# A hand-ordered transformer block with 6,700 pieces in another order: due times per tile and layer

## Chip, core and metric

The kernel runs on one core of one Trainium2 chip. The metric is the device time of one execution in microseconds. A run of the kernel before was measured three times; its median is what a change is compared with.

## What is computed

The input x is 8 sequences of 1024 rows of 256 numbers, in float32. Cut to what matters, the reference is:

```
h = layernorm(x) * (1 + ca) + sa                 # ca, sa, ga, ... from silu(c) @ wmod, per sequence
x = x + ga * attention(h)                        # q, k, v by small products; rope; causal softmax over 1024 rows
h = layernorm(x) * (1 + cb) + sb
for l in range(2):                               # two layers
    s = shift_token(h)                           # columns 128..255 come from the row before
    q, k, v = split(s @ wqkv[l])                 # 8 heads of 64
    q, k = rotary_xpos(l2norm(q) * qs, l2norm(k) * ks)
    h = h + local_attention(q, k, v) @ wo[l]     # windows of 128 rows, each sees itself and the one before
    s = layernorm(shift_token(h)) * lg + lb
    a, g = split(s @ w1[l] + b1[l])
    h = h + (a * gelu(g)) @ w2[l] + b2[l]
x = x + gb * h
```

`shift_token` is the part that the change's DMA edit touches: row r of the second half of the columns is taken from row r - 1.

## The kernel before

A batch is one of the 8 sequences; it is cut into 8 tiles ("windows") of 128 rows. For each batch the kernel runs the causal attention tile by tile, then layer 0, then layer 1 over its 8 windows. Window n counts over everything: n = (2 x batch + layer) x 8 + w. L is 2 x batch + layer, p is a pair of windows (0 to 3).

All work is cut into named pieces, and each engine's program is a list of pieces that it executes strictly in that order. A piece waits for the semaphores of what it reads and of what still reads its buffer, and everything behind it on the engine waits with it. The pieces that matter here:

- Window chain. TensorE: E (three blocks: q, k, v of one window, six float16 matmuls each), F (transposes of q and k), G (scores), H (transposes of probabilities), I (probabilities times v), J (output product). ACT: ev (copy of E out of PSUM), sq, fc, ex (exp), hc, oh. VectorE: x0, x1 (rotary products, L752 and L760), ss (L729), tm (mask and scale, L771), nm (normalisation, L780 and L787), hv (copy, L795), ol (L801), jr (residual add, L807). POOL: pw (power, L889), ad (L893), kk (L899).
- Second half of a layer, by pairs. SP: xs copies the residual's second half of the columns, moved down one row, into the tile XS (L276: 127 rows; L278: the one row that comes from the neighbouring tile). VectorE: ls (statistics, L814 to L819) reads XS, POOL: lt (root, L241 and L243), VectorE: lk (normalised rows XN, L828 and L830), TensorE: N (transposes, L293), ACT: nh, VectorE: nl. Then Wg and Wa (first product), ge, us, uh, ul, and Y (second product, 18 matmuls), yr. D, dh, dl transpose the rows for the next layer.
- Attention. SP: xl loads x. VectorE: st, rw (L627), af; POOL: rt, hl, ra; TensorE: pp (L305), pj, qt, sc, pt, av; VectorE: rp (rope), mx, pc, ys, l2, lr (L710 and L714); POOL: r2.

`schedule()` makes the lists. It gives each piece a due time: the time of its tile (ATTN_TILE, WIN_TILE, MLP_BLOCK, Y_TILE) and an offset of its kind (PAIR_AT, ATTN_AT, WIN_AT, LN_AT, D_AT, MLP_AT), the same for all tiles. Sorting by due time gives each engine's list. The due times have no other use but one: `plan_banks()` goes through TensorE's list and gives each piece the PSUM bank (of 8) whose last user is due to be emptied first. TensorE waits in `claim` until that bank has been emptied. The end of a batch's layer 1 and the attention of the next batch are mixed.

Of the kernel before, what the change touches and what calls it, by code (L numbers as in the profile page):

```python
# [22 lines left out]
P = 128  # L23
EPS = 1e-5
BIG = 1.0e30
BATCH, SEQ, DIM = 8, 1024, 256
NT = SEQ // P
# [4 lines left out]
DEPTH = 2  # L32
# [12 lines left out]
def adaln_kernel(nc, x, w_q, w_k, w_v, wqkv, q_scale, k_scale, wo, ln_g, ln_b, w1, b1, w2, b2,  # L45
# [3 lines left out]
    with ExitStack() as ctx:  # L49
# [29 lines left out]
        X, U = xu[:, 0], xu[:, 1]  # L79
# [27 lines left out]
        uh = [mlp[:, 512 * j:512 * j + 256].bitcast(F16) for j in range(NJ)]  # L107
        ul = [mlp[:, 512 * j + 256:512 * j + 512].bitcast(F16) for j in range(NJ)]
# [9 lines left out]
        ra = ar_c[:, 2048:3072].rearrange("p (r c s n) -> p r c s n", r=2, c=NC, s=2)  # L118
        rb = ar_c[:, 3072:4096].rearrange("p (r c s n) -> p r c s n", r=2, c=NC, s=2)
        XN = sb("XN", [P, 2, 2, DIM])  # L120
        XS = sb("XS", [P, NT, P])
        ot = [sb(f"ot_{s}", [P, 4, P], F16) for s in ("hi", "lo")]
        small = sb("small", [P, 160])
        ss = small[:, 0:32].rearrange("p (r n) -> p r n", r=2)
# [18 lines left out]
        s_xs = [sem(f"shifted_rows{p}") for p in range(DEPTH * NT // 2)]  # L143
# [103 lines left out]
        with block:  # L247

            @block.sync
            def _(sp):  # L250
                for piece in ORDER["sp"]:
                    k = piece[0]
                    if k == "xl":
                        b, p = piece[1:]
                        if b:
                            sp.wait_ge(s_fin, (b - 1) * NT + 2 * p + 2)
                        sp.dma_start(X[:, 2 * p:2 * p + 2, :],
                                     x[b, 2 * p * P:(2 * p + 2) * P, :].rearrange("(t p) d -> p t d", p=P)
                                     ).then_inc(s_x[p], 16)
                    elif k == "mb":  # L260
                        b = piece[1]
                        if b:
                            sp.wait_ge(s_u0, at("lr", b - 1, NT - 1))
                        sp.dma_start(modb[:, :, :],
                                     mod_rows[b, 2 * DIM:5 * DIM].rearrange("(k d) -> k d", k=3).partition_broadcast(P)
                                     ).then_inc(s_mod, 16)
                    elif k == "mg":
                        b = piece[1]
                        if b:
                            sp.wait_ge(s_fa, b * NT)  # L270
                        sp.dma_start(modg[:, :], mod_rows[b, 5 * DIM:6 * DIM].partition_broadcast(P)).then_inc(s_modg, 16)
                    elif k == "xs":
                        n = piece[1]
                        l, w = n // NT % DEPTH, n % NT
                        sp.wait_ge(s_res, at("jr", n))
                        sp.dma_start(XS[1:P, w, :], U[0:P - 1, w, P:DIM]).then_inc(s_xs[l * 4 + w // 2], 16)  # L276
                        if w:
                            sp.dma_start(XS[0:1, w, :], U[P - 1:P, w - 1, P:DIM]).then_inc(s_xs[l * 4 + w // 2], 16)  # L278
                    elif k == "os":
                        b, w = piece[1:]  # L280
                        sp.wait_ge(s_fin, b * NT + w + 1)
                        sp.dma_start(out[b, w * P:(w + 1) * P, :], U[:, w, :]).then_inc(s_out[w], 16)
                for w in range(NT):
                    sp.wait_ge(s_out[w], 16 * NB)

# [623 lines left out]


NB = BATCH

ATTN_TILE = [-0.56, 0.47, 18.59, 31.5, 40.69, 48.66, 54.04, 58.53]
WIN_TILE = [5.09, 15.87, 30.06, 42.77, 56.53, 69.72, 82.93, 95.11]
MLP_BLOCK = [[45.88, 47.36, 49.69, 51.6, 54.17, 56.41], [47.05, 51.59, 53.77, 55.46, 58.12, 61.25]]
Y_TILE = [[65.88, 68.27, 88.1, 92.91], [66.34, 67.28, 73.41, 81.93]]
WIN_START = 8.18
NEXT_WIN = 8.61
NEXT_ATTN = 37.34
PAIR_AT = {"rt": ("pool", -17.04), "st": ("dve", -16.46), "rw": ("dve", -13.71), "pp": ("pe", -13.45),  # L920
           "af": ("dve", -11.85), "hh": ("act", -11.2), "hl": ("pool", -9.56)}
ATTN_AT = {"pj": ("pe", -7.22), "rp": ("dve", -6.0), "vc": ("act", -4.93), "ra": ("pool", -3.82),
           "qt": ("pe", -0.96), "qc": ("act", 0.06), "sc": ("pe", 4.46), "mx": ("dve", 6.39), "pe": ("act", 7.34),
           "av": ("pe", 19.13), "ys": ("dve", 21.78)}
PT_AT = (("pt", "pe", 12.02), ("pc", "dve", 15.4))
LN2_AT = {"l2": ("dve", 23.01), "r2": ("pool", 23.88)}
WIN_AT = {("E", 0): ("pe", -4.18), ("E", 1): ("pe", -2.62), ("E", 2): ("pe", -0.89), ("ev", 0): ("act", -0.67),
# [12 lines left out]
LN_AT = {"ls": ("dve", 38.22), "lt": ("pool", 39.18), "lk": ("dve", 41.9), "N": ("pe", 42.57), "nh": ("act", 43.6),  # L940
         "nl": ("dve", 43.85)}
D_AT = {"D": ("pe", 0.87), "dh": ("act", 4.08), "dl": ("dve", 4.31)}
MLP_AT = {"ge": ("act", 1.8), "us": ("dve", 2.88), "uh": ("act", 3.32), "ul": ("pool", 5.78)}
LR_AT = 27.76
YR_AT = 2.17
D_LAG = -0.53


def schedule():

    made = []

    def put(time, engine, *piece):
        made.append((time, engine, piece))

    a, fin = 30.0, [float(p) for p in range(NT // 2)]
    for b in range(NB):
        A = [a + d for d in ATTN_TILE]
        for p in range(NT // 2):
            put(fin[p], "sp", "xl", b, p)  # L960
            for k, (e, d) in PAIR_AT.items():
                put(A[2 * p] + d, e, k, b, p)
            for k, (e, d) in LN2_AT.items():
                put(A[2 * p + 1] + d, e, k, b, p)
# [4 lines left out]
        for t in range(NT):  # L969
            for k, (e, d) in ATTN_AT.items():  # L970
                put(A[t] + d, e, k, b, t)
            for k, e, d in PT_AT:
                for k4 in range(t // 4 + 1):
                    put(A[t] + d + 0.9 * k4, e, k, b, t, k4)
        s = a + ATTN_TILE[NT - 1] + WIN_START
        d_time = [A[2 * p + 1] + LR_AT + 2.5 for p in range(NT // 2)]
        for l in range(DEPTH):
            L = b * DEPTH + l
            S = [s + d for d in WIN_TILE]
            for p in range(NT // 2):  # L980
# [4 lines left out]
            for w in range(NT):  # L985
                for key, (e, d) in WIN_AT.items():
                    put(S[w] + d, e, key[0], L * NT + w, *key[1:])
            d_time = []
            for g in range(NG):
                m = S[GW * g + GW - 1]  # L990
                for j in range(NJ + 1):
                    put(m + MLP_BLOCK[g][j], "pe", "Wg", L, g, j)
                    if j < NJ:
                        put(m + MLP_BLOCK[g][j] + 1.3, "pe", "Wa", L, g, j)
                    for k, (e, d) in MLP_AT.items():
                        put(m + MLP_BLOCK[g][j] + d, e, k, L, g, j)
                for i in range(GW):
                    y, n = m + Y_TILE[g][i], L * NT + g * GW + i
                    put(y, "pe", "Y", n)
# [6 lines left out]
                if g == 0:  # L1006
                    s_next, a_next = m + Y_TILE[0][0] + NEXT_WIN, m + Y_TILE[0][0] + NEXT_ATTN
            s = s_next
        a = a_next
    made.sort(key=lambda q: q[0])  # L1010
    return ({e: [q for _, g, q in made if g == e] for e in ("sp", "pe", "act", "dve", "pool")},
            {q: time for time, _, q in made})

# [363 lines left out]
```

## Time and profile before

| | |
|---|---|
| median of 3 runs | 3347.26 us (3340.87 to 3353.93) |
| the profiled execution: time, span | 3337.88 us, 3336.1 us |
| granted TensorE clock, mean | 0.939 |
| busy: TensorE, VectorE, ACT, POOL | 2891.3, 2513.0, 1812.7, 1312.5 us |
| instructions: TensorE, VectorE, ACT, POOL | 21580, 7195, 4165, 949 |

All times of a trace are counted from the start of the span. Setup (weights split into a high and a low float16 part) takes the first 110 us or so; then the batches follow at about 400 us each.

### The profile page before, as it was taken

How to read it: one execution, taken by the hardware profiler on the slowest of the kernel's cores; microseconds unless marked ns; L12 is line 12 of the kernel's file. 1: busy time of each engine (PE TensorE's matmuls, PEld its weight loads, DVE VectorE, ACT ScalarE, POOL GpSimd, SP SyncE). 2: the span in 40 equal slices, each digit the busy share in tenths (PEclk: the TensorE clock that was granted, in tenths of full speed). 3: DMA queues.
4: the chain of work that ended last, by engine and by line, in shares of the span. 5: the costliest groups of instructions: out<-in, count | busy, mean ns of one | idle time of the engine just before them, and what ended most of it. 6: DMA issues, size and time to landing. Idle time of an engine off the chain costs nothing.

```text
span 3336.1 us, 63227 instructions
## 1 busy us (share of the span) xinstructions
PE 2891.3 (87%) x21580; PEld 2009.4 (60%) x21580; DVE 2513.0 (75%) x7195; ACT 1812.7 (54%) x4165; POOL 1312.5 (39%) x949
## 2 busy tenths in 40 slices
PE   2489988899888998899979899789988899888997
PEld 2266665666566665566656666566665666556665
DVE  3588777878678786887868878688777978678785
ACT  2146653567536674366734666346653557536673
POOL 1234433544335443344423444344433544335442
PEclk9799999999999999999989999899999999999998
DMA  4100000000000000000000000100000000000000
GB/s 140 33 3 6 4 13 25 4 5 5 22 15 4 5 5 22 14 5 5 5 28 8 5 5 6 33 3 5 5 13 25 4 5 4 22 15 5 4 5 16
DMA packets 57885, 46.22 MB, mean 14 GB/s; under 512 B 18438, under 2 KB 54876, under 8 KB 57444
## 3 DMA queue, kind: packets, MB, share of 16 engines
q1 hardware_dynamic: 53520, 35.14, 3.6%
q10 hardware_dynamic: 4052, 7.04, 0.6%
q8 instruction: 181, 2.97, 0.4%
q14 instruction: 132, 1.08, 0.1%
HBM read 25.33 MB, written 8.44 MB: 10 GB/s over the span
## 4 chain that ended last, share of the span: by engine, by line
PE 55%; DVE 22%; DMA 9%; issue 5%; POOL 3%; ACT 1%; SPq 1%; DVEq 0%; POOLq 0%; ACTq 0%
PE ps L134 11%; PE ps L135 10%; PE ps L136 10%; DMA XS<-xu 8%; PE ps L425 5%; PE ps L410 5%; PE ps L399 4%; DVE ar_b L771 4%; PE ps L334 3%; PE ps L293 2%; DVE small L729 2%; DVE ar_b L787 2%; DVE ar_c L752 2%; PE ps L385 2%; PE ps L353 1%
## 5 line engine op out<-in xcount | busy, mean ns | idle before, releaser
L889 POOL TENSOR_TENSOR small<-small,neg_half 128x16 f32<-128x16 f32 x128 | 391.2, 3056 | 644.5 <-DVE small L734 643.6
L562 ACT ACTIVATE ar_b<-ar_b,small 128x256 f32<-128x256 f32 (+1 forms) x1024 | 492.6, 482 | 113.5 <-DVE small L771 112.0
L771 DVE CUSTOM_DVE_ANT_0 ar_b<-ps,mask_t,small 128x256 f32<-128x256 f32 (+1 forms) x1024 | 413.0, 461 | 12.0 <-PE ps L399 12.0
L410 PE MATMUL ps<-id_f,ar_b 128*128 128x128 f32 x1920 | 280.1, 295 | 102.4 <-DVE ar_b L787 102.3
L787 DVE TENSOR_SCALAR ar_b<-ar_b,rsw 128x256 f32<-128x256 f32 (+1 forms) x1024 | 342.4, 396 | 9.3 <-DVE rsw L780 0.2
L241 POOL TENSOR_SCALAR stats<-stats 128x2 f32<-128x2 f32 x128 | 35.5, 277 | 769.2 <-DVE stats L819 332.7
L410 PEld LDWEIGHTS ps<-id_f,ar_b 128*128 128x128 f32 x1920 | 233.2, 151 | 153.3 <-DVE ar_b L787 137.6
L844 DVE SCALAR_TENSOR_TENSOR mlp<-ps,bias,mlp 128x512 f32<-128x512 f32 x192 | 143.7, 748 | 233.7 <-ACT mlp L592 108.2
L893 POOL TENSOR_TENSOR ar_c<-ar_c 128x1024 f32<-128x1024 f32 x128 | 301.1, 2352 | 20.5 <-DVE ar_c L760 20.5
L908 POOL TENSOR_TENSOR mlp<-mlp 128x512 f16<-128x512 f32 x160 | 193.2, 1208 | 268.3 <-ACT mlp L601 267.3
L134 PE MATMUL ps<-wqkv_hi,ht_hi 128*128 128x512 f16 x768 | 295.9, 385 | 0.0
L135 PE MATMUL ps<-wqkv_lo,ht_hi 128*128 128x512 f16 x768 | 294.8, 384 | 0.0
L136 PE MATMUL ps<-wqkv_hi,ht_lo 128*128 128x512 f16 x768 | 294.2, 383 | 0.0
L134 PE MATMUL ps<-ht_hi,w_hi 128*128 128x512 f16 (+1 forms) x704 | 273.1, 388 | 1.4 <-DVE ht_lo L724 1.4
L135 PE MATMUL ps<-ht_lo,w_hi 128*128 128x512 f16 (+1 forms) x704 | 271.5, 386 | 0.0
L136 PE MATMUL ps<-ht_hi,w_lo 128*128 128x512 f16 (+1 forms) x704 | 269.9, 383 | 0.0
L399 PE MATMUL ps<-ar_a 64*128 64x128 f32 x3840 | 262.8, 289 | 6.8 <-ACT ar_a L552 6.8
L425 PE MATMUL ps<-ar_b,ar_a 128*64 128x128 f32 x3840 | 257.5, 289 | 1.2 <-ACT ar_b L571 1.1
L399 PEld LDWEIGHTS ps<-ar_a 64*128 64x128 f32 x3840 | 236.9, 196 | 33.1 <-issue 24.6
L425 PEld LDWEIGHTS ps<-ar_b,ar_a 128*64 128x64 f32 x3840 | 224.8, 146 | 32.7 <-issue 27.2
L552 ACT ACTIVATE ar_a<-ps 128x512 f32<-128x512 f32 x256 | 148.1, 595 | 104.1 <-PE ps L385 104.0
L571 ACT ACTIVATE ar_b<-ps 128x512 f32<-128x512 f32 (+1 forms) x256 | 144.7, 568 | 100.6 <-PE ps L410 99.5
(171 smaller groups left out, 6837.8 us busy)
## 6 DMA issues: line engine op xcount, KB each, us to landing
xu<-in_L_attn_x_dram SPq DMA_DIRECT2D x32, 256.0 KB, 3.0
out_dram<-xu SPq DMA_DIRECT2D x64, 128.0 KB, 1.7
XS<-xu SPq DMA_DIRECT2D x128, 63.5 KB
ar_a<-in_L_ffn_wqkv_dram ACTq DMA_DIRECT2D x1, 3072.0 KB, 17.1
modb<-mod_rows SPq DMA_DIRECT2D x8, 384.0 KB, 3.5
XS<-xu SPq DMA_DIRECT2D x112, 0.5 KB
ar_a<-in_L_wmod_dram SPq DMA_DIRECT2D x1, 1536.0 KB, 7.5
xu<-in_L_ffn_w_dram SPq DMA_DIRECT2D x1, 1364.0 KB, 9.4
```

The costliest lines, as they stand in the source:

```text
L134: pe.matmul(o, a[0], b[0], start=start, stop=False)
L135: pe.matmul(o, a[0], b[1], start=False, stop=False)
L136: return pe.matmul(o, a[1], b[0], start=False, stop=stop)
L399: last = pe.matmul(ps[:, bk[q], o:o + P], QT[r:r + 64, n % 2, hp, :], KT[r:r + 64, (n - 1 + kb) % 3, hp, :], start=True, stop=True)
L410: last = pe.transpose(ps[:, bk, o:o + P], PW[:, f, q, i, kb * P:(kb + 1) * P], id_f[:])
L425: last = pe.matmul(ps[64 * q:64 * q + 64, bk, (h // 2) * P:(h // 2 + 1) * P], V[:, (n - 1 + kb) % 4, h * DH:(h + 1) * DH], PTW[:, f, q, 2 ...
L562: last = act.activation(pw, pw, ACT.Exp, bias=mnw[:, n % 2, h:h + 1], scale=-1.0, accum_out=smw[:, n % 2, h:h + 1])
L771: last = dve.tensor_tensor_reduce(out=PW[:, f, q, i, c:2 * P], in0=ps[:, bk, i * 256 + c:(i + 1) * 256], in1=mask_t[:, c:2 * P], scale=rin ...
L787: last = dve.tensor_scalar(pw, pw, rsw[:, n % 2, h:h + 1], None, ALU.mult)
L889: pool.tensor_tensor(rinv[:, n % 4, :], ssm[:, n % 2, :], neg_half[:, 0:16], ALU.pow).then_inc(s_rinv, 1)
L893: pool.tensor_tensor(M1[:, n % 2, :], M1[:, n % 2, :], M2, ALU.add).then_inc(s_add, 1)
L908: pool.tensor_tensor(lo, UB[0:rows, v % 2, :], hi, ALU.subtract).then_inc(s_ul, 1)
```

## The change

Three things change; the pieces stay the same ones.

1. Every due time gets a shift of its own, from a table `SHIFT` with an entry for a piece within a batch (by tile for window pieces, by layer and pair or block for the others). The base offsets change as well, and pieces with the same due time (now rounded to 0.01) are sorted by engine and name and no longer in the order in which they were made. All batches get the same shifts.
2. So each engine's list is another order of the same pieces: 2,223 of TensorE's 2,784 pieces stand at another place (by 28 at most), 1,941 of ACT's 2,400, 2,114 of VectorE's 2,720, 346 of POOL's 800 (by 4 at most), 204 of SP's 240. The banks are dealt out anew from the new due times.
3. The step xs of window w no longer fetches its own first row from tile w - 1, but passes the last row of its tile on to tile w + 1. The number of copies is the same, and so is the count that ls waits for.

```diff
                         sp.dma_start(XS[1:P, w, :], U[0:P - 1, w, P:DIM]).then_inc(s_xs[l * 4 + w // 2], 16)
-                        if w:
-                            sp.dma_start(XS[0:1, w, :], U[P - 1:P, w - 1, P:DIM]).then_inc(s_xs[l * 4 + w // 2], 16)
+                        if w + 1 < NT:
+                            sp.dma_start(XS[0:1, w + 1, :], U[P - 1:P, w, P:DIM]).then_inc(s_xs[l * 4 + (w + 1) // 2], 16)
...
-WIN_START = 8.18
-NEXT_WIN = 8.61
-NEXT_ATTN = 37.34
...
-LN_AT = {"ls": ("dve", 38.22), "lt": ("pool", 39.18), "lk": ("dve", 41.9), "N": ("pe", 42.57), "nh": ("act", 43.6),
-         "nl": ("dve", 43.85)}
...
+def in_batch(piece):
+    k, n = piece[0], piece[1]
+    if k in BY_TILE:
+        return (k, n % (DEPTH * NT), *piece[2:])
+    return (k, n % DEPTH, *piece[2:]) if k in BY_LAYER else (k, *piece[2:])
...
+WIN_START = 12.89
+NEXT_WIN = 8.57
+NEXT_ATTN = 38.82
...
+LN_AT = {"ls": ("dve", 41.15), "lt": ("pool", 41.52), "N": ("pe", 43.08), "nl": ("dve", 43.66), "nh": ("act", 44.91),
+         "lk": ("dve", 45.03)}
...
+         ("ls", 0, 3): -5.71, ("ls", 1, 0): 5.18, ("ls", 1, 1): -3.1, ("ls", 1, 2): 1.72, ("ls", 1, 3): 0.76,
...
     def put(time, engine, *piece):
-        made.append((time, engine, piece))
+        made.append((round(time + SHIFT.get(in_batch(piece), 0.0), 2), engine, piece))
...
-    made.sort(key=lambda q: q[0])
+    made.sort()
```

What the sorting gives on VectorE in the first two pairs of a layer 1 (L = 7; the numbers are window, half and quarter), from the residual add jr to the statistics ls:

```
before: jr.57 tm.58.1.0 tm.58.1.1 yr.54 nm.58.0 ls.7.0 nm.58.1 lk.7.0 hv.58.0.0 hv.58.1.0 x0.60 nl.7.0
after:  jr.57 x0.60 ss.60 x1.60 hv.58.0.0 ls.7.0 hv.58.1.0 tm.59.0.1 tm.59.0.0 yr.55 tm.59.1.0 tm.59.1.1 nm.59.0 lk.7.0
before: jr.59 tm.60.1.0 tm.60.1.1 nm.60.0 ls.7.1 nm.60.1 lk.7.1 hv.60.0.0 hv.60.1.0 x0.62 nl.7.1
after:  jr.59 tm.60.1.1 tm.60.1.0 nm.60.0 nm.60.1 ls.7.1 hv.60.0.0 lk.7.1 x0.62 nl.7.0 hv.60.1.0 nl.7.1
```

On TensorE around the last two windows of that layer:

```
before: Y.57 N.7.2 I.62.0 I.62.1 G.63.0 G.63.1 J.62 H.63.0.1 H.63.0.0 H.63.1.0 H.63.1.1 I.63.0 I.63.1 J.63 Y.58 pp.4.0 Y.59 N.7.3 pj.4.0
after:  I.62.0 I.62.1 Y.57 E.63.2 N.7.2 J.62 H.63.0.1 H.63.0.0 H.63.1.1 H.63.1.0 I.63.0 I.63.1 J.63 pp.4.0 Y.58 pj.4.0 Y.59 N.7.3 pj.4.1
```

## Rows read from the trace of the kernel before

**Rows 1.** The page's first part: busy us (share), instructions of each engine.

```profile
PE 2891.3 (87%) x21580; PEld 2009.4 (60%) x21580; DVE 2513.0 (75%) x7195; ACT 1812.7 (54%) x4165; POOL 1312.5 (39%) x949
```

**Rows 2.** Stretches: length; busy PE, PEld, DVE, ACT, POOL; clock; DMA share, GB/s.

```profile
1400.00:1800.00 400.00, 358.49 (x2683) 249.64 (x2684) 307.45 (x888) 223.26 (x517) 161.69 (x114) 0.94 0.03 10
1410.00:1480.00 70.00, 62.22 (x565) 46.36 (x564) 62.76 (x183) 45.40 (x119) 31.14 (x18) 0.95 0.02 5
```

**Rows 3.** Waits of TensorE, 1400 to 1800 us: total us, times, longest.

```profile
PE ps L410 <- DVE ar_b L787: 13.3, 14, 2.7
PE ps L293 <- DVE XN L830: 11.4, 4, 5.0
PE ps L305 <- DVE ar_c L627: 6.4, 2, 4.1
PE ps L385 <- POOL ar_c L899: 3.1, 1, 3.1
...
PE ps L293 <- DVE xu L714: 2.1, 1, 2.1
```

**Rows 4.** The chain that ended last: shares of the span by line.

```profile
PE ps L134 11%; PE ps L135 10%; PE ps L136 10%; DMA XS<-xu 8%; PE ps L425 5%; PE ps L410 5%; PE ps L399 4%; DVE ar_b L771 4%; PE ps L334 3%; PE ps L293 2%; DVE small L729 2%; DVE ar_b L787 2%; DVE ar_c L752 2%; PE ps L385 2%; PE ps L353 1%
```

**Rows 5.** Groups by line: statistics at L814, idle time before them.

```profile
L814 DVE BATCH_NORM_STATS2 stats<-xu 128x6 f32<-128x128 f32 x128 | 36.5, 286 | 101.1 <-DMA XS<-xu 101.1
```

**Rows 6.** Timeline of VectorE around one ls: start us, us, idle before.

```profile
1434.80 1.93 DVE L787 TENSOR_SCALAR ar_b<-ar_b,rsw 128x256 f32<-128x256 f32 x4
1437.99 0.29 DVE L814 BATCH_NORM_STATS2 stats<-xu 128x6 f32<-128x128 f32 x1 [1.27 <-DMA XS<-xu]
...
1439.37 0.88 DVE L787 TENSOR_SCALAR ar_b<-ar_b,rsw 128x256 f32<-128x256 f32 x3
```

**Rows 7.** Timeline of TensorE, its longer waits in one batch.

```profile
1440.57 1.80 PE L410 MATMUL ps<-id_f,ar_b 128*128 128x128 f32 x8 [2.70 <-DVE ar_b L787]
...
1471.06 1.59 PE L410 MATMUL ps<-id_f,ar_b 128*128 128x128 f32 x8 [2.19 <-DVE ar_b L787]
...
1682.26 1.18 PE L410 MATMUL ps<-id_f,ar_b 128*128 128x128 f32 x8 [2.52 <-DVE ar_b L787]
...
1702.31 1.12 PE L293 MATMUL ps<-id_f,XN 128*128 128x128 f32 x4 [5.01 <-DVE XN L830]
```

**Rows 8.** Timeline of SP's queue at the same place.

```profile
1433.08 0.59 SPq L276 DMA_DIRECT2D XS<-xu  x1
1433.72 0.54 SPq L278 DMA_DIRECT2D XS<-xu  x1
```

**Rows 9.** Stretches while the copy is under way and when it has landed.

```profile
1435.00:1435.50 0.50, 0.50 (x4) 0.24 (x3) 0.50 (x2) 0.50 (x3) 0.50 (x1) 1.00 0.09 22
1437.50:1438.00 0.50, 0.37 (x4) 0.14 (x2) 0.01 (x1) 0.50 (x2) 0.00 (x0) 1.00 0.00 0
```

**Rows 10.** Groups by line: VectorE's pieces of the window chain.

```profile
L771 DVE CUSTOM_DVE_ANT_0 ar_b<-ps,mask_t,small 128x256 f32<-128x256 f32 (+1 forms) x1024 | 413.0, 461 | 12.0 <-PE ps L399 12.0
...
L787 DVE TENSOR_SCALAR ar_b<-ar_b,rsw 128x256 f32<-128x256 f32 (+1 forms) x1024 | 342.4, 396 | 9.3 <-DVE rsw L780 0.2
...
L729 DVE TENSOR_REDUCE small<-ar_c 128x16 f32<-128x1024 f32 x128 | 154.8, 1210 | 10.0 <-ACT ar_c L543 10.0
```

**Rows 11.** Chain of waits inside an E: start, us until the next.

```profile
1480.58 0.21 PE ps L134
```

**Rows 12.** Timeline of POOL at the start of a layer.

```profile
1395.01 2.36 POOL L893 TENSOR_TENSOR ar_c<-ar_c 128x1024 f32<-128x1024 f32 x1 [1.31 <-DVE ar_c L760]
1398.81 0.22 POOL L241 TENSOR_SCALAR stats<-stats 128x2 f32<-128x2 f32 x1 [1.44 <-DVE stats L703]
...
1399.80 1.53 POOL L899 TENSOR_TENSOR ar_c<-ar_c,small 128x512 f32<-128x512 f32 x1
```

**Rows 13.** Stretches after two stalls of TensorE.

```profile
1440.50:1446.50 6.00, 5.76 (x50) 5.05 (x52) 5.12 (x10) 2.20 (x5) 0.00 (x0) 0.72 0.00 0
1471.00:1474.50 3.50, 3.44 (x18) 3.11 (x20) 3.36 (x8) 1.30 (x3) 0.00 (x0) 0.57 0.00 0
```

More of the change, by code:

```diff
@@ L911 @@
 NB = BATCH
[L913 to L916, printed above, removed]
-WIN_START = 8.18
-NEXT_WIN = 8.61
-NEXT_ATTN = 37.34
-PAIR_AT = {"rt": ("pool", -17.04), "st": ("dve", -16.46), "rw": ("dve", -13.71), "pp": ("pe", -13.45),
-           "af": ("dve", -11.85), "hh": ("act", -11.2), "hl": ("pool", -9.56)}
@@ L922 @@
[L922 to L927, printed above, removed]
[12 rows of a table removed]
-LN_AT = {"ls": ("dve", 38.22), "lt": ("pool", 39.18), "lk": ("dve", 41.9), "N": ("pe", 42.57), "nh": ("act", 43.6),
-         "nl": ("dve", 43.85)}
@@ L942 @@
[L942 to L946, printed above, removed]
+BY_TILE = ("E", "F", "G", "H", "I", "J", "Y", "ev", "sq", "fc", "ex", "hc", "oh", "ss", "x0", "x1", "tm", "nm", "hv", "ol",
+           "jr", "yr", "pw", "ad", "kk", "xs")
+BY_LAYER = ("D", "N", "Wg", "Wa", "dh", "dl", "nh", "nl", "ls", "lt", "lk", "ge", "us", "uh", "ul")
+def in_batch(piece):
[3 more added lines that the diff above has]
+    return (k, n % DEPTH, *piece[2:]) if k in BY_LAYER else (k, *piece[2:])
@@ new lines @@
+ATTN_TILE = [-0.64, 1.6, 21.99, 38.98, 48.92, 61.23, 67.63, 73.8]
+WIN_TILE = [5.24, 16.02, 29.76, 42.02, 55.85, 69.1, 82.37, 94.55]
+MLP_BLOCK = [[48.18, 47.24, 50.71, 50.97, 55.45, 58.45], [45.14, 51.2, 51.64, 54.6, 56.44, 57.48]]
+Y_TILE = [[65.87, 68.2, 80.44, 89.61], [69.49, 71.26, 77.42, 77.55]]
+WIN_START = 12.89
+NEXT_WIN = 8.57
+NEXT_ATTN = 38.82
+PAIR_AT = {"hh": ("act", -26.64), "st": ("dve", -23.16), "rw": ("dve", -22.9), "rt": ("pool", -21.26),
+           "af": ("dve", -12.61), "hl": ("pool", -11.55), "pp": ("pe", -7.29)}
@@ new lines @@
+ATTN_AT = {"ra": ("pool", -13.17), "rp": ("dve", -9.26), "pj": ("pe", -3.63), "qt": ("pe", -0.51),
+           "qc": ("act", 5.23), "sc": ("pe", 6.99), "vc": ("act", 8.67), "pe": ("act", 11.1), "mx": ("dve", 15.33),
+           "av": ("pe", 21.39), "ys": ("dve", 23.1)}
+PT_AT = (("pt", "pe", 8.59), ("pc", "dve", 17.24))
+LN2_AT = {"r2": ("pool", -7.05), "l2": ("dve", 34.65)}
+WIN_AT = {("xs",): ("sp", -39.35), ("E", 0): ("pe", -4.43), ("E", 1): ("pe", -3.81), ("ev", 1): ("act", -1.19),
[12 rows of a table added]
+LN_AT = {"ls": ("dve", 41.15), "lt": ("pool", 41.52), "N": ("pe", 43.08), "nl": ("dve", 43.66), "nh": ("act", 44.91),
+         "lk": ("dve", 45.03)}
@@ L949, in schedule @@
+D_AT = {"dh": ("act", -2.08), "D": ("pe", 3.83), "dl": ("dve", 6.88)}
+MLP_AT = {"ge": ("act", 0.33), "uh": ("act", 1.98), "us": ("dve", 2.27), "ul": ("pool", 8.19)}
+LR_AT = 31.25
+YR_AT = 3.36
+D_LAG = -2.04
+SHIFT = {("D", 0, 0): 8.86, ("D", 0, 1): -3.37, ("D", 0, 2): -5.63, ("D", 0, 3): 0.61, ("D", 1, 0): -5.8,
[234 rows of a table added]
 def schedule():
```

257 rows, old and new, of tables (SHIFT, WIN_AT) are left out of this document.

## The prediction

> **What bounds the kernel now.** I read the page's busy row first: TensorE is busy for 87% of the span, VectorE for 75%, the others for less [rows 1]. So TensorE sets the time where it has work, and the question is what it waits for. The stretch view of one batch (1400 to 1800 us; batches start about 400 us apart) shows TensorE busy for 358.5 of 400 us, VectorE for 307.5, a clock of 0.94 [rows 2]. So a batch has 41.5 us of TensorE idle time and (1 - 0.94) x 400 = 24 us of clock that was not granted. All that a new order can win lies in these two sums, since no instruction goes away.
>
> The waits of TensorE in that batch name the owners: 13.3 us for VectorE's normalised probabilities (L787, in front of the window transposes "H"), 11.4 us for the normalised rows XN (L830, in front of "N"), 6.4 us for L627 ("pp"), 3.1 us for the rotated keys (L899, in front of "F"), 2.1 us for L714 ("D") [rows 3]. The chain of waits gives 8% of the span to the shifted-row copy XS, and more only to matmul lines [rows 4]. VectorE's own row says that it stood 101.1 us, 64 times, for that copy at L814 ("ls") [rows 5].
>
> The timeline of one such place shows how that reaches TensorE. VectorE finishes the first half of a window's normalisation ("nm", L787), comes to "ls", stands 1.27 us for XS, does "ls", and only then, at 1439.37, begins the second half of the normalisation [rows 6]. TensorE needs that half for its next transposes and stands 2.70 us [rows 7]. It's an order fault: work that was ready was queued behind a wait. The 2.19 us at 1471 is the same place one pair later [rows 7].
>
> **The copy itself.** The 127-row copy is issued at 1433.08, the one-row copy at 1433.72 [rows 8]; "ls" starts at 1437.99 [rows 6], 4.9 us after the first issue. In between, the DMA share is 0.09, nothing by 1437.5 [rows 9], so these packets use about one of 16 engines, one after another. The change takes the one-row copy out of what "ls" waits for. Bounds: 0 (the big copy lands last anyway) to 0.64 us (the second issue). 128 packets in a single file put the one row at 1/128 of the stream, so I take 0. What counts is whether VectorE has 4.9 us of other work between the residual add "jr" and "ls".
> The Trainium skill (DMA: Bandwidth & Descriptors, "Why a DMA increments its semaphore by 16 and not by 1") says that a copy of 127 partitions goes to a single DMA engine; by that rule, too, the term is 0, and the share in the trace agrees. [...]
>
> **The change part by part.** I added the shifts to the due times and sorted, which gives each engine's order. Everything below is per batch; durations are those of [rows 10] and of rows read in the same way (a window's mask-and-scale "tm" 4 x 0.40 per half, "nm" 4 x 0.40, a copy of probabilities "hv" 0.65, "x0"/"x1" 1.2, "ss" 1.2), and an "E" on TensorE is six matmuls of 0.21 to 0.22 us, 1.3 us [rows 11], a "Y" 18 of half that, 2.0 us.
> (a) VectorE work between the odd tile's "jr" and "ls", for the eight pairs of a batch: before 3.4, 3.4, 3.5, 0.4, 3.8, 3.4, 3.5, 1.6 us; after 5.3, 3.2, 5.1, 0.8, 4.5, 5.1, 3.9, 1.5. Both halves of the running "nm" stand ahead of "ls" in 40 of 48 places, 16 before. The three H stalls behind "ls" (2.70, 2.19 and a second one of 2.19) go: 7.1 us. At the one pair where "nm" stays behind, seven blocks of E and F lie ahead of H and hide it.
> (b) "N" (four waits, 11.4 us, the longest 5.01 [rows 3, 7]): pairs 0 and 2 are passed on one window later. In layer 0 the blocks Y, Y, E, D, F, E, G now lie ahead of the fourth N, some 10 us against 7.5: its 1.9 us go, and the third's 2.1. In layer 1 the third N gets 5.3 us more cover but its rows come 4 us later: of 2.4 us, 1.3 go. The last one (5.01) has a chain jr, copy, ls, POOL root, lk of 9.7 us that nothing shortens, but one projection "pj" moves ahead of it: 1.2 go. Sum 6.5.
> (c) The last window's "tm" moves ahead of "ol": of 2.52 + 0.65 us at 1682 [rows 7] I count 2.9.
> (d) "rw" no longer queues behind a rope piece of 1.6 us, and the last input load goes out before two stores: of 6.4 us [rows 3] 2.5.
> (e) At a layer's start the first key product (L899, "kk") waited on POOL behind a root that itself waited 1.44 us for VectorE [rows 12]; after, it stands ahead of that root, and its input "x1" right behind "x0", no longer behind four pieces of attention. It can start at 1397.4, where the sum before it ends, not at 1399.8: 2.4 of the 3.1 us go. The 2.1 us before "D" go because D comes a window's work later. Sum 4.5.
> Sum of the idle time removed: 7.1 + 6.5 + 2.9 + 2.5 + 4.5 = 23.5 us of 41.5.
> (f) Clock. After the stall of 2.70 us the granted clock is 0.72 over 6 us, after the one of 2.19 us 0.57 over 3.5 us [rows 13]: 1.7 and 1.5 us lost, TensorE being on the 1.2 GHz level for a few us. Seven stalls of that size go: 7 x 1.6 = 11.2 us.
> Gross: 34.7 us a batch.
> (g) What comes back. VectorE is busy 62.8 of 70 us in the windows of a layer, as full as TensorE with 62.2 [rows 2], so that stretch can shrink by only 7 us before VectorE is the bound, while (a) and its clock share ask for about 5. And PSUM banks are claimed sooner: by TensorE work between a bank's last use and its next claim, 6 of 2,970 claims had under 2 us before, 128 of 2,971 after (46 of these are pieces that depend on the same copy anyway). Bounds: nothing comes back, or all 34.7. No row prices either end; I take the middle, 17.3.
> Net 17.4 us a batch, 7.8 batches (the last has no successor to mix with): 136 us. The profiled execution took 3337.9 us, 0.3% under the median of 3347.3; 136 us off the latter is **3210 us**.
> Code, data and pieces are otherwise the same; ACT changes its function table 126 times for 142, hidden under TensorE (1.28 us each if that cover were gone).
>
> **Rivals.**
> 1. *VectorE becomes the bound* (13%). For it: 62.8 of 70 us. Then only its own stalls count. With covers as in (a) against 4.9 us, some 7 of the 12.6 us of DMA wait a batch remain, 5.6 x 7.8 = 44 us go: 3303. Against it: over a whole batch it is 14 points emptier than TensorE.
> 2. *Nothing comes back* (12%): 34.7 x 7.8 = 271 us, 3076.
> 3. *Slower: banks* (7%). The 122 added close claims each make TensorE stand until the engine that empties the bank has come round. At the longest wait of that kind shown, 2.70 us [rows 7], 122 x 2.7 = 329 us against 271 won: 3405. It decides from 2.3 us a claim. Against it: a bank is emptied in about 0.6 us once its copy starts. The Trainium skill (TensorE: Matmul & The Clock Gate, "A second HAM failure mode: psum-queue depth-cycling") tells of short idles between groups of matmuls that keep switching the clock; by that rule such claims would cost clock as well. No trace here shows it for claims.
> 4. *It doesn't do what it says* (6%): stalls move along by one piece, the sum stays: 3347, within 0.5%.
>
> **How the numbers follow.** The forecast, some of the gain coming back, has 62%, from 3150 to 3275. Range for 8 in 10: from 3110 (half of case 2's chance left out) to 3325 (case 1 inside; cases 3 and 4 out). A measurement of this kernel tells 0.5% from no change. Faster: 62 + 12 + 13 = 87%; same 6%; slower 7%. The side is firm because the stalls are ready work behind a wait, which the new order visibly parts; the size is soft because of (g).
>
> **What would show it.** Right: "ls" waits in total well under 101 us; H waits of TensorE under half of 102 us over the run; the mean clock above 0.95; batches 380 to 385 us apart; the landing after the first issue still 4.9 us. Right on (g): new waits of TensorE of 1 us or less in front of pieces that had none. Wrong: the copy lands 0.6 us sooner (then (a) was undersized); batches 400 us apart with TensorE's waits under other names (rival 4); VectorE over 90% busy in all windows (rival 1); many waits of over 2 us in front of J, I, H or "pj" for banks (rival 3).

## The result, and the profile after

The changed kernel takes 3022.93 us (median of four runs, 3016.29 to 3024.27) against 3346.05 us (3340.87 to 3353.93) for the kernel before in the same comparison: a ratio of 0.9031, 95% interval 0.9018 to 0.9043. That is 323 us less, where 136 were forecast. The side was right; the time lies below the range (3110 to 3325).

The page of the changed kernel: busy time (its first part), and the first lines of the chain that ended last (its fourth part).

```profile
PE 2762.9 (91%) x21580; PEld 1915.3 (63%) x21580; DVE 2486.9 (82%) x7195; ACT 1772.8 (59%) x4149; POOL 1344.8 (45%) x949
...
PE 67%; DVE 12%; ACT 5%; POOL 4%; issue 4%; DMA 4%; DVEq 0%; ACTq 0%; POOLq 0%
PE ps L134 13%; PE ps L135 12%; PE ps L136 11%; PE ps L399 7%; PE ps L425 7%; PE ps L410 5%; DMA XS<-xu 4%; PE ps L334 3%; PE ps L385 3%; PE ps L353 2%; PE ps L293 2%; DVE ar_b L787 1%; ACT ar_b L562 1%; DVE ar_b L771 1%; POOL small L889 1%
```

TensorE runs the same 21,580 matmuls as in [rows 1], yet is busy 128.4 us less (2891.3 - 2762.9): the mean granted clock rose from 0.939 to 0.985. Its idle time fell from 3336.1 - 2891.3 = 444.8 us to 3020.0 - 2762.9 = 257.1 us, by 187.7. The two are the whole of the 316.1 us by which the spans differ. The copy XS fell from 8% of the chain [rows 4] to 4%.

Stretches of the changed kernel: the batch from 1260 us on, the windows of one of its layers, and the batch from 560 us on (columns as in [rows 2]).

```profile
1260.00:1620.00 360.00, 341.38 (x2690) 237.11 (x2689) 306.92 (x895) 220.01 (x517) 167.38 (x116) 1.00 0.04 12
1290.00:1355.00 65.00, 62.23 (x571) 44.13 (x571) 61.40 (x192) 48.38 (x129) 32.58 (x18) 1.00 0.02 6
...
560.00:920.00 360.00, 341.39 (x2684) 236.58 (x2682) 305.81 (x892) 219.21 (x517) 166.58 (x116) 0.99 0.04 12
```

A batch takes 360 us, not 400 [rows 2] and not the 380 to 385 that the prediction named. VectorE does the same 307 us of work in it. In the 65 us of windows shown it is busy 61.4 us, 94%, while TensorE is busy 62.2 of them.

Waits of TensorE over the whole run, first before (this view was not shown), then after. L1300 and L1547 are the same wait in the setup.

```profile
PE ps L410 <- DVE ar_b L787: 102.3, 106, 2.7
PE ps L293 <- DVE XN L830: 90.7, 32, 5.1
PE ps L305 <- DVE ar_c L627: 83.4, 17, 30.2
PE ps L1300 <- DMA xu<-in_L_ffn_k_scale_dram: 46.1, 1, 46.1
PE ps L385 <- POOL ar_c L899: 24.6, 8, 3.1
```

```profile
PE ps L1547 <- DMA xu<-in_L_ffn_k_scale_dram: 48.3, 1, 48.3
PE ps L305 <- DVE ar_c L627: 42.0, 9, 30.1
PE ps L293 <- DVE XN L830: 23.4, 8, 4.5
PE ps L134 <- POOL ht_lo L872: 19.5, 17, 2.9
PE ps L385 <- POOL ar_c L899: 14.4, 8, 2.0
PE ps L399 <- ACT ar_a L552: 14.2, 24, 0.8
```

The wait for the normalised probabilities (L787), the largest before, is gone from this list: the groups by line give it 9.2 us. And the statistics ls, which stood 101.1 us 64 times [rows 5], stand 34.4 us. The groups by line of the changed kernel:

```profile
L771 DVE CUSTOM_DVE_ANT_0 ar_b<-ps,mask_t,small 128x256 f32<-128x256 f32 (+1 forms) x1024 | 419.3, 462 | 36.2 <-PE ps L399 35.5
L787 DVE TENSOR_SCALAR ar_b<-ar_b,rsw 128x256 f32<-128x256 f32 (+1 forms) x1024 | 304.4, 360 | 9.1
L410 PE MATMUL ps<-id_f,ar_b 128*128 128x128 f32 x1920 | 268.7, 275 | 9.6 <-DVE ar_b L787 9.2
...
L814 DVE BATCH_NORM_STATS2 stats<-xu 128x6 f32<-128x128 f32 x128 | 36.3, 283 | 34.7 <-DMA XS<-xu 34.4
```

How the copy is covered can be read in VectorE's timeline. The residual add is at 1308.41; both halves of the normalisation, a copy and a rotary product follow, and ls (L814) starts 5.46 us after the add with no wait.

```profile
1308.41 0.42 DVE L807 TENSOR_TENSOR xu<-ps,xu 128x256 f32<-128x256 f32 x1 [0.20 <-PE ps L136]
1308.75 0.17 DVE L780 RECIPROCAL rsw<-small 128x4 f32<-128x4 f32 x1
1308.95 1.14 DVE L787 TENSOR_SCALAR ar_b<-ar_b,rsw 128x256 f32<-128x256 f32 x4
1310.01 0.17 DVE L780 RECIPROCAL rsw<-small 128x4 f32<-128x4 f32 x1
1310.22 2.00 DVE L787 TENSOR_SCALAR ar_b<-ar_b,rsw 128x256 f32<-128x256 f32 x4
1312.14 0.68 DVE L795 COPY ar_b<-ps 128x512 f32<-128x512 f32 x1
1312.74 1.21 DVE L752 TENSOR_TENSOR ar_c<-ar_b,xp_t 128x1024 f32<-128x1024 f32 x1
1313.87 0.28 DVE L814 BATCH_NORM_STATS2 stats<-xu 128x6 f32<-128x128 f32 x1
```

One pair later the cover is short and ls waits 1.54 us, with the normalisation behind it. First SP's queue, then VectorE, then TensorE, in their timelines:

```profile
1333.41 0.60 SPq L276 DMA_DIRECT2D XS<-xu  x1
...
1338.16 0.30 DVE L814 BATCH_NORM_STATS2 stats<-xu 128x6 f32<-128x128 f32 x1 [1.54 <-DMA XS<-xu]
...
1339.42 1.14 DVE L787 TENSOR_SCALAR ar_b<-ar_b,rsw 128x256 f32<-128x256 f32 x4
...
1340.62 0.66 PE L410 MATMUL ps<-id_f,ar_b 128*128 128x128 f32 x4 [0.35 <-DVE ar_b L787]
```

From issue to ls it is 4.75 us, against 4.91 before [rows 6, 8]. Over all the places where ls waits, the median is 4.76 us after (32 places) and 4.93 before (64). The place costs TensorE 0.35 us where the same fault cost 2.70 [rows 7], since blocks of E and F now lie in front of H.

### The profile page after: what moved, and what is told of

Same layout as the page of the kernel before. It is cut to its first block, busy times and chain, and to the rows that moved or that the text cites. A ratio compares the mean times of both kernels' runs of the same rounds, so it can differ in the third digit from the quotient of the medians.

```text
span 3020.0 us, 63211 instructions
## 1 busy us (share of the span) xinstructions
PE 2762.9 (91%) x21580; PEld 1915.3 (63%) x21580; DVE 2486.9 (82%) x7195; ACT 1772.8 (59%) x4149; POOL 1344.8 (45%) x949
## 4 chain that ended last, share of the span: by engine, by line
PE 67%; DVE 12%; ACT 5%; POOL 4%; issue 4%; DMA 4%; DVEq 0%; ACTq 0%; POOLq 0%
PE ps L134 13%; PE ps L135 12%; PE ps L136 11%; PE ps L399 7%; PE ps L425 7%; PE ps L410 5%; DMA XS<-xu 4%; PE ps L334 3%; PE ps L385 3%; PE ps L353 2%; PE ps L293 2%; DVE ar_b L787 1%; ACT ar_b L562 1%; DVE ar_b L771 1%; POOL small L889 1%
## 5 line engine op out<-in xcount | busy, mean ns | idle before, releaser
L889 POOL TENSOR_TENSOR small<-small,neg_half 128x16 f32<-128x16 f32 x128 | 406.2, 3174 | 432.5 <-DVE small L734 430.7
L771 DVE CUSTOM_DVE_ANT_0 ar_b<-ps,mask_t,small 128x256 f32<-128x256 f32 (+1 forms) x1024 | 419.3, 462 | 36.2 <-PE ps L399 35.5
L893 POOL TENSOR_TENSOR ar_c<-ar_c 128x1024 f32<-128x1024 f32 x128 | 301.7, 2357 | 227.5 <-DVE ar_c L760 227.0
L787 DVE TENSOR_SCALAR ar_b<-ar_b,rsw 128x256 f32<-128x256 f32 (+1 forms) x1024 | 304.4, 360 | 9.1
L241 POOL TENSOR_SCALAR stats<-stats 128x2 f32<-128x2 f32 x128 | 29.9, 234 | 598.0 <-DVE stats L819 253.2
L399 PE MATMUL ps<-ar_a 64*128 64x128 f32 x3840 | 270.5, 282 | 14.2 <-ACT ar_a L552 14.2
L410 PE MATMUL ps<-id_f,ar_b 128*128 128x128 f32 x1920 | 268.7, 275 | 9.6 <-DVE ar_b L787 9.2
L908 POOL TENSOR_TENSOR mlp<-mlp 128x512 f16<-128x512 f32 x160 | 208.5, 1311 | 125.2 <-ACT mlp L601 123.8
L425 PE MATMUL ps<-ar_b,ar_a 128*64 128x128 f32 x3840 | 245.0, 277 | 3.1 <-DVE ar_b L795 2.0
L410 PEld LDWEIGHTS ps<-id_f,ar_b 128*128 128x128 f32 x1920 | 216.6, 141 | 43.7 <-DVE ar_b L787 22.9
L425 PEld LDWEIGHTS ps<-ar_b,ar_a 128*64 128x64 f32 x3840 | 206.6, 137 | 34.0 <-issue 14.8
L844 DVE SCALAR_TENSOR_TENSOR mlp<-ps,bias,mlp 128x512 f32<-128x512 f32 x192 | 140.4, 743 | 97.3 <-ACT mlp L592 47.8
L562 ACT ACTIVATION_READ_ACCUMULATOR ar_b<-ar_b,small 128x1 f32 x1024 | 193.3, 189 | 0.0
## 6 DMA issues: line engine op xcount, KB each, us to landing
XS<-xu SPq DMA_DIRECT2D x128, 63.5 KB
```

The costliest lines, as they stand in the source:

```text
L399: last = pe.matmul(ps[:, bk[q], o:o + P], QT[r:r + 64, n % 2, hp, :], KT[r:r + 64, (n - 1 + kb) % 3, hp, :], start=True, stop=True)
L410: last = pe.transpose(ps[:, bk, o:o + P], PW[:, f, q, i, kb * P:(kb + 1) * P], id_f[:])
L425: last = pe.matmul(ps[64 * q:64 * q + 64, bk, (h // 2) * P:(h // 2 + 1) * P], V[:, (n - 1 + kb) % 4, h * DH:(h + 1) * DH], PTW[:, f, q, 2 ...
L562: last = act.activation(pw, pw, ACT.Exp, bias=mnw[:, n % 2, h:h + 1], scale=-1.0, accum_out=smw[:, n % 2, h:h + 1])
L771: last = dve.tensor_tensor_reduce(out=PW[:, f, q, i, c:2 * P], in0=ps[:, bk, i * 256 + c:(i + 1) * 256], in1=mask_t[:, c:2 * P], scale=rin ...
L787: last = dve.tensor_scalar(pw, pw, rsw[:, n % 2, h:h + 1], None, ALU.mult)
```

## Experiments

Each is compared with the kernel before in the same comparison (3342.08 to 3344.55 us, and 3346.05 in the one above). A difference between two variants is taken from their medians, so a few us between variants of different comparisons tell nothing.

### ls behind the normalisation, in the kernel before

```diff
-LN_AT = {"ls": ("dve", 38.22), "lt": ("pool", 39.18), "lk": ("dve", 41.9),
+LN_AT = {"ls": ("dve", 39.1), "lt": ("pool", 39.18), "lk": ("dve", 41.9),
```

> Kernel before, one due time changed: ls stands behind both halves of nm in all 48 places (16 before). Theory A (stalls are ready work behind a wait, and removing them is worth their idle time plus the clock they cost): at most 7.1 + 4.8 us a batch, 95 us, less what lk now waits for the root on POOL right behind ls (1 us in two thirds of the places); 3265 to 3310 us, TensorE's waits for L787 fall from 102 us to under 60, clock above 0.95. Theory B (half of it comes back as other waits, as my term (g) had it): 3300 to 3330. Rival (a stall removed alone only moves to the next piece; the gain needs the joint order): 3340 to 3350, waits for L787 fall and others rise by as much.

Measured: 3308.63 us, ratio 0.9894 [0.9873, 0.9915], 36 us less than before, where the ranges of theories A and B overlap; the clock, 0.946, stayed under the 0.95 of theory A. Both halves of nm now stand ahead of ls in all 48 places. (In the last pair of a layer 1, ls also falls behind one piece of attention.) TensorE's waits in the whole run:

```profile
PE ps L293 <- DVE XN L830: 138.5, 64, 5.0
PE ps L305 <- DVE ar_c L627: 82.4, 17, 29.9
PE ps L1300 <- DMA xu<-in_L_ffn_k_scale_dram: 48.2, 1, 48.2
PE ps L410 <- DVE ar_b L787: 43.0, 83, 2.5
```

The wait for L787 falls by 59.3 us and the wait for XN rises by 47.8: what is moved back delays the rows that N needs. Between the two profiled executions the span falls by 24.6 us, of which 20.0 are busy time (2871.3 for 2891.3) and only 4.6 are idle time. So for this single edit in an otherwise fixed order most of the idle time does come back. The next experiment moves lk back too.

```diff
-LN_AT = {"ls": ("dve", 39.1), "lt": ("pool", 39.18), "lk": ("dve", 41.9),
+LN_AT = {"ls": ("dve", 39.1), "lt": ("pool", 39.18), "lk": ("dve", 43.2),
```

> As b_ls, and lk behind the copies hv, so that POOL's root is covered too; but the rows XN are ready 1 to 2 us later. Theory A: no VectorE wait for the root, more gain than b_ls at the H stalls, but up to 1.5 us more in front of each N: 3260 to 3310. If N is what counts, slower than b_ls by 10 to 40 us.

Measured: 3341.99 us, ratio 1.0003 [0.9991, 1.0014]. That is as slow as the kernel before. The H gain is there (L787 costs 44.3 us) and the wait for XN takes it back whole:

```profile
PE ps L293 <- DVE XN L830: 157.7, 64, 5.3
```

### ls in front of the normalisation, in the changed kernel

```diff
+    order = {e: [q for _, g, q in made if g == e] for e in ("sp", "pe", "act", "dve", "pool")}
+    dve = order["dve"]
+    for ls in [q for q in dve if q[0] == "ls"]:
+        i = dve.index(ls)
+        near = [j for j in range(i - 3, i) if dve[j][0] == "nm"]
+        if near:
+            dve.insert(near[-1], dve.pop(i))
```

> Changed kernel with the opposite edit: wherever nm stands within three pieces ahead of ls, ls is put in front of it, so that both halves of nm are ahead of ls in 8 of 48 places (40 in the changed kernel). Theory A: VectorE's wait for the copy rises from 34 us to about 34 + 40 x 1.7 = 100 us and two or three H stalls a batch come back with their clock: 3060 to 3110. Rival (the rest of the new order has slack enough, the place of ls is not what carries the gain): under 3040.

Measured: 3125.88 us, ratio 0.9346 [0.933, 0.9361], 103 us above the changed kernel and 16 us above the range of theory A. nm stands ahead of ls in 8 places instead of 40. The groups by line:

```profile
L410 PE MATMUL ps<-id_f,ar_b 128*128 128x128 f32 x1920 | 281.4, 284 | 83.0 <-DVE ar_b L787 82.3
...
L293 PE MATMUL ps<-id_f,XN 128*128 128x128 f32 x256 | 40.4, 281 | 23.4 <-DVE XN L830 23.4
```

The wait for L787 goes from 9.2 to 82.3 us and XN stays at 23.4. That one wait is all of the new idle time (+73 us; the spans differ by 104.2), and the busy time rises by 30.9 us at a clock of 0.978. A third of the gain hangs on this one order, in which 32 places changed: 3.2 us each.

### The form of the copy

```diff
-                        if w + 1 < NT:
-                            sp.dma_start(XS[0:1, w + 1, :], U[P - 1:P, w, P:DIM]).then_inc(s_xs[l * 4 + (w + 1) // 2], 16)
+                        if w:
+                            sp.dma_start(XS[0:1, w, :], U[P - 1:P, w - 1, P:DIM]).then_inc(s_xs[l * 4 + w // 2], 16)
```

> Changed kernel, but xs fetches its own first row again, so that ls waits for the one-row copy issued 0.64 us after the big one. Theory A (both go through one DMA engine, one behind the other, the row is 1/128 of the stream): 3018 to 3028, ls starts as late after the first issue as before, 4.9 us. Rival (the second issue delays the landing by its 0.64 us, and all 64 places feel it): 64 x 0.64 = 41 us at most, 3040 to 3064.

Measured: 3025.75 us, ratio 0.9047 [0.9033, 0.906]: 2.8 us above the changed kernel, and the intervals overlap. ls waits 43.4 us for 34.4, and from issue to ls the median is 4.93 us again (48 places), as in the kernel before. So the one row costs about 0.17 us a place, not nothing, and its later issue costs far less than 0.64. TensorE's waits rise by 6 us in all (250.0 to 256.2): little of it reaches TensorE.

### How close a bank is claimed

The two kernels keep their orders; only the table of banks changes, dealt out so that the bank emptied last is taken first.

```diff
+BANKS = (
+    "00200203103301344534251453162145125240425602435254232443545543260456231642073161730671067601276721030176310623"
...
-        k = min(range(9 - wide), key=lambda i: max(until[i:i + wide]))
+        k = int(BANKS[len(bank)])
```

> Kernel before, same order of all pieces, PSUM banks dealt out so that a claim takes the bank emptied last: 706 claims come under 2 us of TensorE work after the bank's last use (6 before, 128 in the changed kernel). Theory 'close claims cost' (my rival 3 and part of my term g): at even 0.5 us each 350 us more, at 0.1 us 70 us more. Theory 'the bank is empty by then and closeness alone costs nothing': 3335 to 3360.

> Changed kernel, same order, banks dealt out in the same way: 556 close claims for 128. Theory 'close claims cost': the 428 added ones at 0.1 to 0.5 us, 3065 to 3240. Theory 'nothing': 3010 to 3040.

Measured: the order of before 3377.5 us, ratio 1.0106 [1.0089, 1.0122], with 706 claims under 2 us instead of 6: +35 us, 0.05 us each. The new order 3066.02 us, ratio 0.9174 [0.9159, 0.919], with 556 such claims instead of 128: +43 us, 0.10 us each. The sum of TensorE's waits rises by 48 us in the one (439.5 to 487.1) and 36 in the other (250.0 to 285.9). The first time lies between the two theories, the second at the lower edge of 'close claims cost'. At these averages the 122 added claims of the change would cost some 6 to 12 us in the whole run, an estimate, against 2.3 us each from which rival 3 would have decided. The granted clock did not fall: 0.948 for 0.939 and 0.988 for 0.985. The Trainium skill (TensorE: Matmul & The Clock Gate, "A second HAM failure mode: psum-queue depth-cycling") tells of short idles between matmul groups that keep switching the clock. By it these runs could have lost clock; no run here shows that.

> Changed kernel, same order, banks dealt out so that a claim takes the one emptied first: 91 close claims for 128. At the 0.05 to 0.10 us a claim that b_recent and a_recent showed: 2 to 4 us less, 3019 to 3023; if the dealing of before (from due times) left real waits behind, up to 15 us less, 3008.

Here the banks are dealt by another rule, with 91 close claims for 128. Measured: 3032.46 us, ratio 0.9066 [0.9051, 0.908], 9.5 us slower than the changed kernel where it was expected to be level or faster. So the number of close claims alone doesn't set the price: another dealing with fewer of them cost time as well. Which claims cost, and why, is not shown.

### Where in a batch the gain lies

A part of the pieces keeps the order of before. In the first kernel the new order holds only in the windows (from the first projection of a batch's layer 0 to its last output product), in the second only in the rest, where attention and the second half of layer 1 are mixed. SP keeps its old order in both, and both take their banks from a table of their own. Of the 6,624 pieces that the change moves on the other four engines, 5,648 (85%) are moved in the first kernel and 976 in the second.

> New order on TensorE, ACT, VectorE and POOL only for the windows of both layers (from the first x0 of a batch to the last J), the order of before for the mixed stretch (Y.58 on, attention of the next batch); SP as before. By my sum the windows hold (a) 7.1, (b) without the last N 5.3, (c) 2.9 and (e) 4.5, 19.8 of 23.5 us of idle time a batch, and 6 of 7 clock terms. Theory A (the parts add): of the 323 us it takes 85%, 275 us, 3070. Theory B (the parts need each other): under half, above 3185.

> The complement: new order only in the mixed stretch at the end of a batch, windows as before. Theory A: 15%, about 50 us, 3295; with h_win it adds up to 323 us. Theory B: no gain, or a sum of the two far from 323 us.

Measured: windows alone 3114.03 us, ratio 0.9321 [0.9303, 0.934], 228 us less than before; the rest alone 3276.89 us, ratio 0.9807 [0.9787, 0.9826], 65 us less. With the windows alone, L787 costs TensorE 13.6 us and XN 36.7; with the rest alone they cost 96.2 and 65.4. So the windows give 71% of the gain, between theory A's 85% and theory B's half, and the rest gives 20% with 15% of the moved pieces. The remaining 30 us come only with both, with SP's new order or with the banks as `plan_banks()` deals them; these were not told apart (a table of its own cost 9.5 us in the experiment before).

### Which engine bounds the changed kernel

In the first kernel the E blocks have two products instead of three, in the second only half of each nm is done.

```diff
-                            last = mm3(pe, ps[:, bk, :], [q[:, c, a:a + P] for q in ht],
-                                       [q[:, L % DEPTH, c, s * INNER:(s + 1) * INNER] for q in wqkv_p], c == 0, c == 1)
+                            pe.matmul(ps[:, bk, :], hh[0], ww[0], start=(c == 0), stop=False)
+                            last = pe.matmul(ps[:, bk, :], hh[0], ww[1], start=False, stop=(c == 1))
```

```diff
-                            for i in range(2):
+                            for i in range(1):
```

> Changed kernel without the third product (low part of the activations by high part of the weights) of each E block, 2 of 6 matmuls: 384 x 2 x 0.215 = 165 us less work on TensorE, nothing else. Leaves that product out. If TensorE is what bounds the changed kernel: 2858 to 2900. If VectorE (61.4 of 65 us busy in the windows) is the bound that my term (g) took it for: under a third of it, 2970 to 3020.

> Changed kernel with two of the four normalisations of each nm left out: 512 x 0.36 = 184 us less work on VectorE (and the transposes H ready 0.7 us sooner). Leaves half the probabilities unnormalised. If VectorE is the bound in the windows: 2840 to 2930. If TensorE is: 2990 to 3020.

Measured: with less TensorE work 2990.18 us, ratio 0.8936 [0.892, 0.8952], 33 us under the changed kernel; with less VectorE work 3006.14 us, ratio 0.8987 [0.8971, 0.9004], 17 us under it. The pages' busy times, TensorE's work cut first:

```profile
PE 2639.8 (88%) x20812; PEld 1840.3 (62%) x20812; DVE 2485.1 (83%) x7195; ACT 1771.6 (59%) x4149; POOL 1340.3 (45%) x949
```

```profile
PE 2748.1 (92%) x21580; PEld 1912.6 (64%) x21580; DVE 2353.8 (78%) x6683; ACT 1772.8 (59%) x4149; POOL 1336.5 (45%) x949
```

TensorE's busy time fell by 123 us (165 were meant), and 92 us came up as new idle time. Its waits (lines are one higher in this kernel):

```profile
PE ps L386 <- POOL ar_c L900: 40.0, 21, 3.9
PE ps L293 <- DVE XN L831: 39.1, 24, 4.6
PE ps L411 <- DVE ar_b L788: 38.5, 93, 1.4
```

These were 14.4, 23.4 and 9.2 us. So the chains through POOL and VectorE run only just behind TensorE: with 27% of its cut work won (33 of 123 us), TensorE is not what bounds the kernel alone, and by the written expectation the time falls on the side of VectorE. But VectorE, 94% busy in those windows, gave back an eighth of the 133 us by which its busy time fell, and by its own expectation that time falls on the side of TensorE. Nearly all of these 17 us are clock: TensorE's busy time fell by 14.8 us, its idle time by 2.9. Neither engine alone sets the time; the order makes them wait for each other. Rival 1, VectorE as the only bound, is out.

### POOL's order

The changed kernel with POOL's list of before; all other lists are the new ones. 346 of its 800 pieces stand elsewhere, by 4 places at most.

> Changed kernel with POOL's list of before (346 of 800 pieces move back, by 4 at most); all other lists and banks new. My term (e) gave the place of kk ahead of the root r2 2.4 us a batch. Theory A (POOL's list matters at that place and little else): 3040 to 3070. Rival (POOL is 45% busy and its order is free): 3015 to 3030. A joint order that needs its POOL list: above 3100.

Measured: 3225.32 us, ratio 0.9641 [0.9625, 0.9656], 202 us above the changed kernel. That is the third of the written expectations, a joint order that needs its POOL list. I had 2.4 us a batch for POOL's order, about 19. TensorE's waits:

```profile
PE ps L385 <- POOL ar_c L899: 124.3, 40, 7.5
PE ps L134 <- POOL ht_lo L872: 54.2, 16, 6.7
```

The wait for the rotated keys (kk, L899) is 124.3 us in 40 places, where the changed kernel has 14.4 in 8 and the kernel before has 24.6 in 8. POOL's timeline in this kernel shows one cause: a root of the statistics (L241), which itself waits for VectorE, stands in front of the power and the keys of a window.

```profile
1390.31 1.04 POOL L899 TENSOR_TENSOR ar_c<-ar_c,small 128x512 f32<-128x512 f32 x1
1397.53 0.22 POOL L241 TENSOR_SCALAR stats<-stats 128x2 f32<-128x2 f32 x1 [6.18 <-DVE stats L819]
1397.84 0.71 POOL L243 TENSOR_TENSOR stats<-stats,neg_half 128x2 f32<-128x2 f32 x1
1399.41 3.27 POOL L889 TENSOR_TENSOR small<-small,neg_half 128x16 f32<-128x16 f32 x1 [0.86 <-DVE small L734]
```

POOL is 42% busy there and the cost is still two thirds of the whole gain. In the kernel before, the same list stands beside other lists and the keys cost 24.6 us. A POOL piece that is ready behind one that waits for a moved VectorE piece is the same order fault, one engine on.

Not tried: the new list of one engine alone in the kernel before, and the shifts set to zero or averaged over the tiles. So what the shifts, the core of the change, are worth beyond the new base offsets stays open.

## Why the prediction was wrong in size

The step that failed is **(g)**, that half of the gross gain comes back: 135 us were taken off, and 58.5 us of idle time came back, 77 less. The gross sum was low as well, by 65 us of idle time and by 41 us of clock **(f)**. To rounding, these three are the 182 us between the forecast gain and the measured one. Over the run the two lists of TensorE's waits give, by releaser, what went away (before - after) beside 7.8 batches of the forecast:

| step | forecast, us | measured, us |
|---|---|---|
| (a) and (c), L787 | 78 | 102.3 - 9.2 = 93.1 |
| (b), XN | 51 | 90.7 - 23.4 = 67.3 |
| (d), L627 | 20 | 83.4 - 42.0 = 41.4 |
| (e), kk and D | 35 | 10.2 + 21.6 = 31.8 |
| other waits that shrank | 0 | 14.4 |
| idle time gone | 183 | 248.0 |
| (f), clock (measured: net) | 87 | 128.4 |
| (g), come back (measured: idle time only) | -135 | -58.5 |
| net | 136 | 318 (span: 316) |

- **(a)** Right in mechanism: b_ls and a_ls move the wait of L787 by 59 and 73 us with this order alone, and the pair that I said would stay uncovered cost 0.35 us. The term of the copy's form, put at 0, measured 0.17 us a place.
- **(b), (d)** Undersized. Of the four waits for XN a batch, three went whole, and the last one, with one projection more in front of it, kept 2.7 us of its 5.0, where I had left 3.8. The waits for L627 fell by about 5 us a batch, where I had 2.5.
- **(e)** The keys gained half of what I said, the transposes D all of it and more. I took POOL's reordering for a matter of a batch's start. It is also what keeps kk in time at the other places (40 of them wait in a_old_pool). These are waits that would have arisen under the other new lists and didn't, so no row of before could show them.
- **(f)** I gave clock back for seven stalls, at 1.6 us each, what went missing in 3.5 to 6 us behind two of them. Stretches of the kernel before, 10 us long, behind the stalls at 1702 and 1682 [rows 7]:

```profile
1702.30:1712.30 10.00, 9.90 (x43) 5.41 (x44) 6.10 (x22) 3.48 (x6) 2.54 (x2) 0.76 0.23 82
1682.20:1692.20 10.00, 7.87 (x59) 6.70 (x60) 4.54 (x14) 2.17 (x5) 0.13 (x1) 0.66 0.15 47
```

That is 2.4 and 3.4 us that went missing in two places. 11.2 + 5.8 = 17.0 us a batch, and a batch's busy time fell by 358.5 - 341.4 = 17.1, but this agreement is luck: the stall at 1682 is the one of (c) and of the size of my seven, and behind what is left of the one at 1702 the changed kernel still loses 1.6 us:

```profile
1547.10 1.11 PE L293 MATMUL ps<-id_f,XN 128*128 128x128 f32 x4 [2.71 <-DVE XN L830]
...
1547.00:1557.00 10.00, 9.90 (x45) 5.20 (x45) 6.52 (x25) 4.15 (x6) 2.54 (x2) 0.84 0.15 43
```

Over the run 128.4 us of busy time went with 187.7 of idle time, 0.7 us a microsecond, against my 0.48. The experiments don't confirm that as a rate: 0.7 in h_win (93.6 for 132.0), but 0.4 in a_ls (30.9 for 73.3), 0.3 in a_old_pool (49.2 for 154.7), and in b_recent the busy time fell by 8 us while the idle time rose by 48. Where the idle time changed little, the busy time changed by more (h_mix 36.6 for 26.0, b_ls 20.0 for 4.6). Which stalls cost how much clock stays open.
- **(g)** What came back in new or longer waits is 58.5 us (2.2 of them in the setup), in pieces of about 1 us as I said they would look: ht_lo L872 5.8 to 19.5, ar_a L552 6.8 to 14.2, L877 5.2 to 10.5, and several under 7. For it I had named a nearly full VectorE and close bank claims. The runs price them: 17 us for 133 less of VectorE work (a_dvelight), an estimated 6 to 12 us for the claims. A single edit gives back even more than half (of the idle time b_ls gave back 48 of 59 us, b_ls2 everything). This change moves lk, N and POOL's pieces along. That this is why so little comes back is shown for POOL's list (a_old_pool); for lk and N it is argued, not shown. I had no row for either end and took the middle. My own count of covers over N and kk was evidence for the upper end, and I didn't use it.
- **Rivals.** 2 (nothing comes back, 3076) was nearest and had 12%. The time is below even that, because of (f) and the undersized idle terms. 1 is refuted as it was priced (3303 us) and by a_dvelight, but VectorE did become as tight as TensorE; over a batch it was 13 points emptier before (307.5 for 358.5 of 400 us), not 14. 3 is refuted by b_recent and a_recent, 4 by the batch of 360 us.
- **What would show it.** ls waits 34.4 us, H waits 9.2 and clock 0.985 came as named; the batch distance didn't (380 to 385 named, 360 measured). VectorE over 90% busy in the windows, my sign for rival 1, came too in the stretch shown (94%), without the time of rival 1: the busy share alone was no sign of a bound.

How the gain splits among the lists can't be told by adding: lists taken back one at a time cost 103 us (ls alone), 202 us (POOL's), out of 323. They can't be taken as independent shares.

## What to carry to other kernels

Price a reordering by its stalls twice, as idle time and as the clock that is lost behind them (here from nothing to 0.7 us for every microsecond of idle time, in the runs where that changed by over 30 us, so as a range). In this case a single moved piece gave back most of what it won, while a joint move of all lists kept three quarters of its idle time: before giving back half, look whether the pieces behind the moved one move with it. And judge an engine's list by who waits for its pieces, not by its busy share.

## What was not expected of the hardware

- Dealing the PSUM banks so that 706 and 556 of some 2,970 claims come less than 2 us of TensorE work after the bank's last use cost 35 and 43 us, with no loss of granted clock: 0.05 to 0.10 us a claim on average.
- L787, 1,024 instructions alike, took 396 ns each before [rows 10] and 360 ns after. Its own time didn't change: with nothing on POOL beside it, one of full width takes 348 ns in both kernels. Beside POOL's instructions at L893, L899 or L908 it takes up to 1.3 us: 124 times before, 775 ns on average, and 56 times after, 714 ns on average. That is 33 of the 37 us by which its 1,024 durations shrank in sum. In VectorE's timeline above, the four at 1308.95 take 1.14 us and the four at 1310.22 take 2.00, with this on POOL:

```profile
1310.76 1.04 POOL L899 TENSOR_TENSOR ar_c<-ar_c,small 128x512 f32<-128x512 f32 x1
```

POOL's L889, with 16 columns, doesn't stretch it (349 ns). With POOL's list of before in the changed kernel (a_old_pool) the mean is 394 ns again. So where POOL's pieces fall also sets how long VectorE's last.
- The 127-row copy of 63.5 KB took 4.72 us in the chain of waits, from issue to landing:

```profile
1333.41 4.72 DMA XS<-xu
1338.13 0.02 issue
1338.16 0.30 DVE stats L814
```
